# Adaptive FFN with experts: the low parts of h ahead of the turns of its rows

## The chip, the cores and the metric

The kernel runs on one core of one Trainium2 chip. The metric is the device time of one execution in microseconds. Five engines work side by side and meet at semaphores: TensorE (PE in the rows) multiplies 128x128 weights by up to 512 columns, VectorE (DVE) and ScalarE (ACT) work on tiles, GpSimd (POOL) does a little arithmetic and the indirect transfers, and SyncE (SP) issues the other DMAs in the order in which they are written.

## The reference

The input x has 8192 tokens of 512 numbers (128 batches of 64 tokens). Cut to what is computed:

```python
q_emb = relu(q @ W3 + b3)                                  # one row per batch
v_sum = sum(v, axis=1)
h = relu(((n * v + v_sum) * q_emb) @ W2 + b2)              # conditioned tokens
scores = softmax(h @ gate_w.T); topk_w, topk_i = top_k(scores, 6)      # 64 experts
buf = each expert's first 64 tokens (capacity 64), rows of h
y = (silu(buf @ w_gate) * (buf @ w_up)) @ w_down           # per expert, width 352
shared = (silu(h @ sw_gate) * (h @ sw_up)) @ sw_down       # all tokens, width 704
out = x + sum of y * weight over a token's experts + shared
```

## The kernel before, in words

**Precision.** A float32 product is made of three products in a shorter format: a value v is split into a high part (ScalarE's rounding copy) and a low part (VectorE's subtraction, `lower`, L743), and `three` (L1102 to L1104) adds high x high, high x low and low x high. For h these parts are `hh` and `hl`, each of four quarters `oc` of 128 features by the 512 tokens of a chunk.

**Stages.** The tokens are 16 chunks of 512. The first stage has a prologue (chunk 0, and the splitting of the shared weights, with GpSimd's part at L531) and eight bodies. A body `i` treats chunks b = 2i + 1, c = 2i + 2 and prepares d = 2i + 3; only the odd chunks' shared expert is done here, the even ones' follow in the second stage, beside the 32 pairs of experts. For each chunk:

- TensorE turns x (`transpose_x`, L1112); VectorE makes the conditioned input (`take_xt`, L764 to L783) and `xml` (`split_xm`), ScalarE `xmh`.
- TensorE multiplies by W2, one quarter of the features at a time (`cond_tile`, 48 matmuls a chunk in four tiles of 12). ScalarE takes each tile as h, relu and bias (`take_cond`, L597), and copies it to `hh`.
- VectorE turns each quarter of h into rows (`take_rows`, L796) for the table in DRAM from which the experts gather, and makes `hl` (`split_h`).
- TensorE multiplies h by the gate weights (`logits_raw`, L1136 and L1137, 8 matmuls of 512 columns), ScalarE copies the result to `lsb` (`take_lraw`), TensorE turns it (`logits`, L1147), and VectorE's `route` (L847 to L864) finds the six experts. `score` (L870 to L873) makes their weights from ScalarE's exp.
- For odd chunks, eleven gate and up tiles (`gu_tile`), with silu on ScalarE and `product` (L810) and `split_a` on VectorE between them, then four down tiles (`down_tile`, 17 matmuls each), which VectorE adds to x (`take_down`, L827 in this stage), and SP stores.
- The candidates of a body's two chunks are merged into each expert's first 64 in eight rounds (`merge`, L885 and L888, the last with L890).

**Order.** Everything is written out by hand: each engine's `body(i)` lists its steps, and its queue runs them strictly in that order. A step waits on semaphores for the others; a tile of PSUM is used again when its reader has signalled. SP's queue is in order too: a DMA that waits holds up all behind it. A TensorE unit at the high clock takes about 12 x 0.23 us for a `cond_tile` or `gu_tile`.

**What the prediction's steps touch.** VectorE's `split_h` and `body`; the opening lines of VectorE's queue; TensorE's `logits_raw`, called in the prologue for chunk 0 and in a body for b and for c; SP's `body`. ScalarE's `take_cond(n, oc)` waits for the turn and the low part of the same quarter of the chunk before, since h, `hh` and `hl` have one buffer each. The turned rows have one buffer as well (`hrow`): the first turn of a chunk waits until SP's stores of the last rows have landed, and `store_rows` waits for all four turns. `load_xr(v, j)` brings x for the sum of `take_down`, and has to wait until the buffer's last output is stored.

Of the kernel before, what the change touches and what calls it, by code (L numbers as in the profile page):

```python
# [21 lines left out]
def adaln_moe_ffn_kernel(nc, x, cond, W3, b3, W2, b2, gate_w, w_gate, w_up, w_down,  # L22
# [12 lines left out]
    NCH = T // CH  # L35
    J = CH // P
    KC = D // P
# [27 lines left out]
    with ctx:  # L65
# [26 lines left out]
        hh = keep("hh", [P, KC, CH], F32R)  # L92
        hl = keep("hl", [P, KC, CH], F32R)
# [253 lines left out]
        def _(sp):  # L347
# [95 lines left out]
            def body(i):  # L443
# [17 lines left out]
                if c < NCH:  # L461
                    store_hT(c // 2)
                    store_rows(c)
                    store_out(i, 0)
                    load_xr(i, 2)
                    store_out(i, 1)
                    keep_x(c)
# [273 lines left out]
        def _(dve):  # L741
# [57 lines left out]
            def split_h(n, oc):  # L799
                if n < NCH:  # L800
                    take_rows(n, oc)
                dve.wait_ge(s.hh_ready, KC * n + oc + 1)
                lower(hl[:, oc, :], h32[:, oc, :], hh[:, oc, :]).then_inc(s.hl_ready, 1)
# [92 lines left out]
            def body(i):  # L896
# [5 lines left out]
                score(a)  # L902
                split_h(b, 2)
                if i > 0:
                    merge(i - 1, 5)
                split_h(b, 3)
                if i > 0:
                    merge(i - 1, 6)
                    take_down(v - 1, 3)
                    merge(i - 1, 7)  # L910
                if not more:
# [37 lines left out]
                split_xm(d, 3)  # L949
                take_down(v, 0)  # L950
                take_down(v, 1)
                take_down(v, 2)

            def last_half(i):
# [90 lines left out]
            dve.wait_ge(s.pads_stored, 32)  # L1045
            split_h(0, 0)
            split_h(0, 1)
            take_xt(1, 2)
            split_h(0, 2)
            split_h(0, 3)  # L1050
            for j in range(J):
# [48 lines left out]
        def _(pe):  # L1100
# [29 lines left out]
            def logits_raw(n):  # L1130
                pe.wait_ge(s.hh_ready, KC * (n + 1))
                pe.wait_ge(s.hl_ready, KC * (n + 1))
                pe.wait_ge(s.cond_taken, KC * n + 3)
                o = bank[5]
                for k in range(KC):
                    nc.tensor.matmul(o[:, :], gw2[:, k, :], hl[:, k, :], start=(k == 0), stop=False)  # L1136
                    op = nc.tensor.matmul(o[:, :], gw2[:, k, :], hh[:, k, :], start=False, stop=(k == KC - 1))  # L1137
                op.then_inc(s.lraw_filled, 1)
# [242 lines left out]
```

## Time and profile before

| | us |
|---|---|
| median of 3 runs (range) | 1303.83 (1303.19 to 1304.71) |
| profiled execution | 1304.96 |
| its span | 1303.2 |
| TensorE busy in the span | 1262.3 (97%) |
| VectorE busy | 729.9 (56%) |
| ScalarE busy | 336.9 (26%) |
| TensorE idle before `logits_raw` | 18.4 |
| mean granted clock of TensorE, share of full | 0.986 |

The span is the time between the first and the last instruction; the rest of the profiled execution lies around it. Busy time of matmuls overlaps, so 97% is not the peak; what can be read from it is where TensorE is not busy. The first stage ends near 663 us, the second takes the rest.

### The profile page before, as it was taken

The page shows a single profiled execution, that of the slowest core. Times are in us where ns is not written, and L with a number is a line of the kernel's source. Part 1 is how long each engine was busy: PE and PEld are TensorE (multiplying, and loading weights), DVE is VectorE, ACT ScalarE, POOL GpSimd, SP SyncE. Part 2 cuts the span into 40 slices and gives each one's busy share as a digit, 9 for nine tenths or more (in the row PEclk, how much of TensorE's full clock was granted, in tenths as well). Part 3 has the DMA queues.
Part 4 walks back from the last instruction along what each step waited for, and adds up shares of the span by engine and source line. Part 5 has one row for each costly group of instructions (what it writes and reads, how often), then busy time and mean ns, then how long its engine had stood idle before and what let it go on. Part 6 is the DMA issues. An engine that isn't in the chain of part 4 may idle for free.

```text
span 1303.2 us, 15965 instructions
## 1 busy us (share of the span) xinstructions
PE 1262.3 (97%) x6104; PEld 935.7 (72%) x6104; DVE 729.9 (56%) x1524; ACT 336.9 (26%) x547; POOL 171.1 (13%) x129
## 2 busy tenths in 40 slices
PE   4879999999999999999999999999999999999999
PEld 3668888888888888887876666676666667666666
DVE  6789797979978797896743223232232232323322
ACT  3534233233424333342312011121121111211111
POOL 3320000000000000000001222222222222222221
PEclk7889999999999999999999999999999999999999
DMA  5531605344161532605755997987979889898852
GB/s 196 168 117 51 195 23 178 90 125 142 37 183 48 174 93 81 187 9 164 284 202 194 287 316 217 323 295 241 312 263 315 287 260 314 243 305 286 288 134 77
DMA packets 121453, 250.91 MB, mean 193 GB/s; under 512 B 18016, under 2 KB 50912, under 8 KB 119200
## 3 DMA queue, kind: packets, MB, share of 16 engines
q1 hardware_dynamic: 109888, 224.71, 51.0%
q0 software_dynamic: 11488, 25.17, 9.6%
q8 instruction: 49, 0.80, 0.2%
q14 instruction: 28, 0.23, 0.1%
HBM read 197.14 MB, written 61.10 MB: 198 GB/s over the span
## 4 chain that ended last, share of the span: by engine, by line
PE 96%; issue 2%; ACT 1%; DMA 1%; DVE 0%; SPq 0%
PE bank L1102 23%; PE bank L1104 22%; PE bank L1103 22%; PE bank L1300 12%; PE bank L1323 7%; PE bank L1112 2%; PE bank L1136 2%; PE bank L1137 1%; PE bank L1282 1%; PE bank L1197 1%; PE bank L1196 1%; PE bank L1309 1%; DMA stage<-in_L_cond_W_dram 1%; PE bank L1147 1%; ACT w2h L581 0%
## 5 line engine op out<-in xcount | busy, mean ns | idle before, releaser
L1102 PE MATMUL bank<-hh,gu 128*128 128x512 f32 x704 | 281.8, 400 | 0.0
L1104 PE MATMUL bank<-hh,gu 128*128 128x512 f32 x704 | 275.0, 391 | 0.0
L1103 PE MATMUL bank<-hl,gu 128*128 128x512 f32 x704 | 274.7, 390 | 0.0
L1102 PEld LDWEIGHTS bank<-hh,gu 128*128 128x128 f32 x704 | 132.8, 189 | 38.2 <-issue 12.8
L810 DVE TENSOR_TENSOR prod<-bank,prod 128x512 f32<-128x512 f32 x96 | 66.3, 690 | 165.7 <-PE bank L1104 139.6
L1104 PEld LDWEIGHTS bank<-hh,gu 128*128 128x128 f32 x704 | 132.3, 188 | 28.6
L1103 PEld LDWEIGHTS bank<-hl,gu 128*128 128x128 f32 x704 | 132.6, 188 | 25.4
L1102 PE MATMUL bank<-sdh,ah 128*128 128x512 f32 x320 | 126.8, 396 | 0.0
L581 ACT ACTIVATE ah<-prod 128x512 fp32r<-128x512 f32 x96 | 60.6, 632 | 251.3 <-DVE prod L810 251.3
L1103 PE MATMUL bank<-sdl,ah 128*128 128x512 f32 x320 | 124.7, 390 | 0.0
L1104 PE MATMUL bank<-sdh,al 128*128 128x512 f32 x320 | 124.7, 390 | 0.0
L536 POOL DMA_INDIRECT hg<-table,idx_pair x32 | 33.0, 1032 | 684.1 <-DVE idx_hi L1025 588.8
L1102 PE MATMUL bank<-xmh,w2h 128*128 128x512 f32 x256 | 103.7, 405 | 2.2 <-DVE xml L743 1.3
L617 ACT ACTIVATE prod<-bank 128x512 f32<-128x512 f32 x96 | 57.0, 594 | 172.4 <-PE bank L1104 172.2
L1104 PE MATMUL bank<-xmh,w2l 128*128 128x512 f32 x256 | 101.0, 395 | 0.0
L1103 PE MATMUL bank<-xml,w2h 128*128 128x512 f32 x256 | 100.9, 394 | 0.0
L1323 PE MATMUL bank<-wd,eactT 128*64 128x512 f32 (+1 forms) x384 | 89.6, 601 | 0.0
L1079 DVE TENSOR_SCALAR ysc<-bank,hg 64x512 f32<-64x512 f32 x64 | 48.0, 750 | 61.2 <-PE bank L1323 53.9
L1300 PE MATMUL bank<-wg,hgt 128*64 128x352 f32 x512 | 81.3, 459 | 0.0
L1300 PE MATMUL bank<-wu,hgt 128*64 128x352 f32 x512 | 81.2, 459 | 0.0
L597 ACT ACTIVATE h<-bank,b2c 128x512 f32<-128x512 f32 x64 | 44.0, 687 | 133.0 <-PE bank L1104 133.0
L1060 DVE TENSOR_TENSOR eact<-bank,esilu 128x352 f32<-128x352 f32 x32 | 16.8, 525 | 102.4 <-issue 96.4
(117 smaller groups left out, 1726.5 us busy)
## 6 DMA issues: line engine op xcount, KB each, us to landing
wg<-in_L_ffn_w_gate_dram SPq DMA_DIRECT2D x64, 704.0 KB, 8.0
wu<-in_L_ffn_w_up_dram SPq DMA_DIRECT2D x64, 704.0 KB, 10.3
wd<-in_L_ffn_w_down_dram SPq DMA_DIRECT2D x64, 512.0 KB
x<-in_x_dram SPq DMA_DIRECT2D x16, 1024.0 KB, 8.3
table<-hrow SPq DMA_DIRECT2D x64, 256.0 KB, 4.3
wd<-in_L_ffn_w_down_dram SPq DMA_DIRECT2D x64, 192.0 KB
out_dram<-outst SPq DMA_DIRECT2D x36, 256.0 KB, 4.5
hT<-h SPq DMA_DIRECT2D x8, 1024.0 KB, 3.9
```

What stands on the lines that cost most here:

```text
L536: nc.gpsimd.indirect_dma_start(out=hg[p % 3][:, :], out_offset=None, in_=table, in_offset=bass.IndirectOffsetOnAxis(ap=idx_pair[:, p:p + 1 ...
L581: return nc.scalar.activation(o, i, ACT.Copy)
L597: nc.scalar.activation(h32[:, oc, :], bank[5 + oc % 2][:, :], ACT.Relu, bias=b2c[:, oc:oc + 1]).then_inc(s.cond_taken, 1)
L617: nc.scalar.activation(prod[0:m, i % 2, :], bank[t % 3][0:m, :], ACT.Silu).then_inc(s.silu_ready, 1)
L810: nc.vector.tensor_tensor(prod[0:m, i % 2, :], bank[t % 3][up0:up0 + m, :], prod[0:m, i % 2, :], ALU.mult).then_inc(s.prod_ready, 1)
L1079: op = nc.vector.tensor_scalar(ysc[p % 3][rows, :], bank[6][rows, :], hg[p % 3][rows, at:at + 1], None, ALU.mult)
L1102: nc.tensor.matmul(o, st_h, mv_h, start=first_mm, stop=False)
L1103: nc.tensor.matmul(o, st_h, mv_l, start=False, stop=False)
L1104: return nc.tensor.matmul(o, st_l, mv_h, start=False, stop=last_mm)
L1112: op = nc.tensor.transpose(bank[3 + j % 2][:, k * P:(k + 1) * P], x32[:, n % 2, j, k * P:(k + 1) * P], ident[:, :])
L1300: op = nc.tensor.matmul(o[half, 0:I], hgt[:, k, half], w[p % 2][e][:, k * I:(k + 1) * I], start=(k == 0), stop=(k == KC - 1))
L1323: op = nc.tensor.matmul(bank[6][half, :], eactT[0:m, it, half], wd[e][0:m, it, :], start=(it == 0), stop=(it == IT - 1))
```

## The change

It has three parts. In `logits_raw` TensorE's four matmuls with `hh` come first, and each of the four with `hl` has a wait of its own. On VectorE `take_rows` is no longer part of `split_h`: in both halves of a body the four turns follow the four low parts, in the first half directly, in the second half after `take_down(v, 0)`; in the prologue the order stays as it was. Rounds 5, 6 and 7 of merging move from the first half of the next body to the end of the body, between and behind the down tiles. On SP `store_rows(c)` goes behind `load_xr(i, 2)`.

```diff
@@ SP, body
                 if c < NCH:
                     store_hT(c // 2)
-                    store_rows(c)
                     store_out(i, 0)
                     load_xr(i, 2)
+                    store_rows(c)
                     store_out(i, 1)
@@ VectorE, split_h
             def split_h(n, oc):
-                if n < NCH:
-                    take_rows(n, oc)
                 dve.wait_ge(s.hh_ready, KC * n + oc + 1)
@@ VectorE, body, first half
                 split_h(b, 2)
+                split_h(b, 3)
+                for oc in range(KC):
+                    take_rows(b, oc)
                 if i > 0:
-                    merge(i - 1, 5)
-                split_h(b, 3)
-                if i > 0:
-                    merge(i - 1, 6)
                     take_down(v - 1, 3)
-                    merge(i - 1, 7)
@@ VectorE, body, second half
                 take_down(v, 0)
+                for oc in range(KC):
+                    take_rows(c, oc)
                 take_down(v, 1)
+                merge(i, 5)
+                merge(i, 6)
                 take_down(v, 2)
+                merge(i, 7)
@@ TensorE, logits_raw
                 pe.wait_ge(s.hh_ready, KC * (n + 1))
-                pe.wait_ge(s.hl_ready, KC * (n + 1))
                 pe.wait_ge(s.cond_taken, KC * n + 3)
                 o = bank[5]
                 for k in range(KC):
-                    nc.tensor.matmul(o[:, :], gw2[:, k, :], hl[:, k, :], start=(k == 0), stop=False)
-                    op = nc.tensor.matmul(o[:, :], gw2[:, k, :], hh[:, k, :], start=False, stop=(k == KC - 1))
+                    nc.tensor.matmul(o[:, :], gw2[:, k, :], hh[:, k, :], start=(k == 0), stop=False)
+                for k in range(KC):
+                    pe.wait_ge(s.hl_ready, KC * n + k + 1)
+                    op = nc.tensor.matmul(o[:, :], gw2[:, k, :], hl[:, k, :], start=False, stop=(k == KC - 1))
```

TensorE, the product for chunk 0 with the instructions beside it, before (gw_67 is the gate weights, xmh and w2h are operands of `cond_tile`):

```order
L1104 MATMUL bank<-xmh,w2l 128x512
L1136 MATMUL bank<-hl,gw_67 128x512 [waits cond_taken,hl_ready,hh_ready]
L1137 MATMUL bank<-hh,gw_67 128x512
L1136 MATMUL bank<-hl,gw_67 128x512
L1137 MATMUL bank<-hh,gw_67 128x512
L1136 MATMUL bank<-hl,gw_67 128x512
L1137 MATMUL bank<-hh,gw_67 128x512
L1136 MATMUL bank<-hl,gw_67 128x512
L1137 MATMUL bank<-hh,gw_67 128x512
L1102 MATMUL bank<-xmh,w2h 128x512 [waits lraw_taken,cond_taken,xml_ready,xmh_ready]
```

and now:

```order
L1105 MATMUL bank<-xmh,w2l 128x512
L1136 MATMUL bank<-hh,gw_67 128x512 [waits cond_taken,hh_ready]
L1136 MATMUL bank<-hh,gw_67 128x512 x3
L1139 MATMUL bank<-hl,gw_67 128x512 [waits hl_ready] x4
L1103 MATMUL bank<-xmh,w2h 128x512 [waits lraw_taken,cond_taken,xml_ready,xmh_ready]
L1104 MATMUL bank<-xml,w2h 128x512
```

The wait for hl stood ahead of all eight; it now stands ahead of each of the last four.

VectorE, first half of body 0, chunk 1, from the end of its `route` to `take_xt` of chunk 2, before (hrow is the buffer of turned rows, h_54 is h, ez the exp):

```order
L796 STREAM_TRANSPOSE hrow<-h_54 128x512
L743 TENSOR_TENSOR hl<-h_54,hh 128x512
L796 STREAM_TRANSPOSE hrow<-h_54 128x512
L743 TENSOR_TENSOR hl<-h_54,hh 128x512
L870 TENSOR_REDUCE ssum<-ez 128x4
L871 RECIPROCAL rsum<-ssum 128x4
L873 TENSOR_TENSOR sc<-ez,rsum 128x256
L796 STREAM_TRANSPOSE hrow<-h_54 128x512
L743 TENSOR_TENSOR hl<-h_54,hh 128x512
L796 STREAM_TRANSPOSE hrow<-h_54 128x512
L743 TENSOR_TENSOR hl<-h_54,hh 128x512
L764 TENSOR_REDUCE vsum<-bank 128x8 x2
```

and now:

```order
L743 TENSOR_TENSOR hl<-h_54,hh 128x512 x2
L868 TENSOR_REDUCE ssum<-ez 128x4
L869 RECIPROCAL rsum<-ssum 128x4
L871 TENSOR_TENSOR sc<-ez,rsum 128x256
L743 TENSOR_TENSOR hl<-h_54,hh 128x512 x2
L796 STREAM_TRANSPOSE hrow<-h_54 128x512 x4
L764 TENSOR_REDUCE vsum<-bank 128x8 x2
```

The four turns have left the places ahead of the low parts and stand together behind the last of them.

VectorE, second half of body 0, chunk 2, from the last two quarters to the down tiles and the next `route`, before (outst is the output buffer of `take_down`):

```order
L796 STREAM_TRANSPOSE hrow<-h_54 128x512
L743 TENSOR_TENSOR hl<-h_54,hh 128x512
L796 STREAM_TRANSPOSE hrow<-h_54 128x512
L743 TENSOR_TENSOR hl<-h_54,hh 128x512
L743 TENSOR_TENSOR xml<-xm,xmh 128x4x128 x2
L743 TENSOR_TENSOR xml<-prod,xmh 128x4x128 x2
L827 TENSOR_TENSOR outst<-bank,outst 128x512 x3
L847 COPY lg<-bank 128x256
```

and now (first and cand are the merge's buffers):

```order
L743 TENSOR_TENSOR hl<-h_54,hh 128x512 x2
L743 TENSOR_TENSOR xml<-xm,xmh 128x4x128 x2
L743 TENSOR_TENSOR xml<-prod,xmh 128x4x128 x2
L825 TENSOR_TENSOR outst<-bank,outst 128x512
L796 STREAM_TRANSPOSE hrow<-h_54 128x512 x4
L825 TENSOR_TENSOR outst<-bank,outst 128x512
L883 MAX first<-cand 128x8
L886 MATCH_REPLACE cand<-first,cand 128x576
L883 MAX first<-cand 128x8
L886 MATCH_REPLACE cand<-first,cand 128x576
L825 TENSOR_TENSOR outst<-bank,outst 128x512
L883 MAX first<-cand 128x8
```

The turns of chunk c stand between the first two down tiles, two merge rounds between the next two, and the last round behind the third.

## Rows read from the trace of the kernel before

**Rows 1.** The page: shares of the span along the chain that ended last, by engine.

```profile
PE 96%; issue 2%; ACT 1%; DMA 1%; DVE 0%; SPq 0%
```

**Rows 2.** TensorE's waits: line, releaser, total us, times, longest us.

```profile
PE bank L1136 <- issue: 18.4, 10, 8.4
```

**Rows 3.** TensorE in time order: start us, duration us, instruction, [idle before, releaser]; the opening.

```profile
47.43 0.76 PE L1136 MATMUL bank<-hl,gw 128*128 128x512 f32 x1 [5.45 <-issue]
...
52.07 0.76 PE L1102 MATMUL bank<-xmh,w2h 128*128 128x512 f32 x1 [0.89 <-ACT lsb L581]
...
74.64 0.77 PE L1136 MATMUL bank<-hl,gw 128*128 128x512 f32 x1 [8.42 <-issue]
...
78.19 0.63 PE L1102 MATMUL bank<-hh,gu 128*128 128x512 f32 x1
...
81.56 0.60 PE L1147 MATMUL bank<-ident,lsb 128*128 128x128 f32 x4
...
87.49 1.03 PE L1112 MATMUL bank<-ident,x 128*128 128x128 f32 x8
```

**Rows 4.** TensorE in time order, around the product for chunk 4, body 1.

```profile
203.53 0.39 PE L1196 MATMUL bank<-sdh,ah 128*128 128x512 f32 x1
203.76 0.39 PE L1197 MATMUL bank<-sdl,ah 128*128 128x512 f32 x1
204.68 0.47 PE L1136 MATMUL bank<-hl,gw 128*128 128x512 f32 x1 [0.53 <-issue]
...
206.60 0.40 PE L1102 MATMUL bank<-sdh,ah 128*128 128x512 f32 x1
```

**Rows 5.** ScalarE and VectorE in time order, second half of body 1 and after.

```profile
201.06 0.63 ACT L581 ACTIVATE hh<-h 128x512 fp32r<-128x512 f32 x1
...
203.91 0.67 DVE L743 TENSOR_TENSOR hl<-h,hh 128x512 fp32r<-128x512 f32 x1
...
214.71 0.69 DVE L827 TENSOR_TENSOR outst<-bank,outst 128x512 f32<-128x512 f32 x1 [3.35 <-DMA outst<-in_x_dram]
...
217.68 0.42 DVE L847 COPY lg<-bank 128x256 f32<-128x256 f32 x1 [2.29 <-PE bank L1147]
...
220.46 0.69 ACT L597 ACTIVATE h<-bank,b2c 128x512 f32<-128x512 f32 x1
...
227.37 0.73 DVE L885 MAX8 first<-cand 128x8 f32<-128x576 f32 x1
```

**Rows 6.** Stretches: us, TensorE busy (matmuls), granted clock, DMA share, GB/s.

```profile
52.00:56.00 4.00, 3.93 (x10) 0.55 0.14 31
...
72.00:76.00 4.00, 1.36 (x3) 0.50 0.25 56
...
79.00:80.00 1.00, 1.00 (x5) 0.77 1.09 189
```

**Rows 7.** VectorE and ScalarE in the opening; last, GpSimd's L531: count, min/median/max ns, starts.

```profile
48.44 1.28 DVE L743 TENSOR_TENSOR xml<-prod,xmh 128x512 fp32r<-128x512 f32 x2
...
65.72 3.47 DVE L873 TENSOR_TENSOR sc<-ez,rsum 128x256 f32<-128x256 f32 x1
66.10 0.63 ACT L581 ACTIVATE hh<-h 128x512 fp32r<-128x512 f32 x1
...
69.11 1.08 DVE L796 STREAM_TRANSPOSE hrow<-h 128x512 f32<-128x512 f32 x1
70.04 2.98 DVE L743 TENSOR_TENSOR hl<-h,hh 128x512 fp32r<-128x512 f32 x1
...
L531 POOL TENSOR_TENSOR sdl<-stage,sdh x2: 3430/3521/3612, 65.5 to 68.9; 128x1536 fp32r<-128x1536 f32 x2
```

**Rows 8.** VectorE in body 0: `take_xt` of chunk 2, `route` of chunk 1, first product.

```profile
74.46 0.67 DVE L764 TENSOR_REDUCE vsum<-bank 128x8 f32<-128x512 f32 x1
...
82.20 0.42 DVE L847 COPY lg<-bank 128x256 f32<-128x256 f32 x1 [3.93 <-PE bank L1147]
...
86.90 0.69 DVE L810 TENSOR_TENSOR prod<-bank,prod 128x512 f32<-128x512 f32 x1
```

More of the change, by code:

```diff
@@ L1045, in _ @@
             dve.wait_ge(s.pads_stored, 32)
[L1046 to L1050, printed above, removed]
+            for oc in range(KC):
+                take_rows(0, oc)
+                split_h(0, oc)
+                if oc == 1:
+                    take_xt(1, 2)
             for j in range(J):
```

## The prediction, made before the changed kernel ran

> **What bounds the kernel now.** I read the page first. The chain that ended last is 96% TensorE [rows 1], so time is won only where TensorE waits or runs at its lower clock, and lost only where it starts to wait. The table of what TensorE waited for comes next: of its 1303.2 us it sat idle before the product of h with the gate weights (`logits_raw`, L1136) for 18.4 us in 10 cases [rows 2], and it lists no other wait after the one of 0.89 us ahead of 52.07 [rows 3], so none at all in the second stage. TensorE's timeline gives the cases: 5.45 us ahead of 47.43 (chunk 0), 8.42 us ahead of 74.64 (chunk 1) [rows 3], and eight short ones that make up the rest, 18.4 - 5.45 - 8.42 = 4.5 us: one in each of the seven bodies for chunk c, like the 0.53 ahead of 204.68 [rows 4], which make 3.7, and one for chunk 15, 0.8. The releaser is called "issue", but the matmul waits for the last piece of hl: VectorE's subtraction (L743) of 203.91 is the last before 204.68 [rows 5]. Last I asked for the granted clock by stretch: it is 0.50, which is 1.2 GHz, in the stretch from 72 to 76, and the mixed values 0.55 and 0.77 say that it came back to 2.4 GHz near 55.5 and near 79.5 [rows 6]. After each long wait TensorE worked for a while at the lower of its two clocks.
>
> **The change, part by part.**
>
> *TensorE's order in `logits_raw`.* The same eight matmuls; the four with hh go first and want only hh, then each hl matmul waits for its own quarter. No work added. Four waits are added where one stood; behind each stands all of TensorE's queue.
>
> *First product, chunk 0.* VectorE's order stays (turn, then low part, per quarter), so hl is complete when it was, just before 47.43. TensorE is free at 47.43 - 5.45 = 41.98 [rows 3], does the hh and two hl matmuls during the old wait, and the last two by about 47.8. Before, the product ended near 51, and `cond_tile(1, 0)` began at 52.07, when ScalarE had copied the logits. Now that copy is done near 48.6 and the next wait is what decides: xml of chunk 1, done at 48.44 + 1.28 = 49.7 [rows 7]. So that tile starts 2.3 us earlier, not 3.3. What those 2.3 us are worth hangs on the clock. At the low clock one 128x512 matmul takes 0.43 us of the queue (74.64 to 78.19 for eight, the first a little longer), at the high one 0.23 (203.53 to 203.76) [rows 3, 4]. The clock came back here at about 55.5 [rows 6]. If it comes back at the same moment, 2.3 us at the low clock are 5.4 matmuls, worth 5.4 x 0.23 = 1.2 us. If it never falls, TensorE does (55.5 - 49.8) / 0.23 = 25 matmuls by 55.5 instead of 8, worth 3.9. If the return comes later than it did, as little as 0.3. TensorE still stands idle for most of the time from 42 to 49.8, as it did before the clock was found low, so I take **1.2**.
>
> *Second product, chunk 1.* Here the order on VectorE changes. Before: a turn of 1.08 (0.93 from start to start, 69.11 to 70.04) stands ahead of each low part, and score (`sc`, L873) came at 65.72, just after GpSimd had begun its two subtractions of 3.43 and 3.61 us at 65.5 and 68.9; it took 3.47 instead of 0.42. The low part at 70.04 took 2.98 instead of 0.67, while the turn at 69.11, amid the second one, kept its 1.08 [rows 7]. Now, in the old time scale: route ends at 62.0 (65.72 less two turns, two low parts and two small instructions, 0.93, 0.6 and 0.3 apart), hl 0 and 1 run at 62.0 to 63.3, score ends by 64.3 and hl 2 by 65.0, all before GpSimd starts. hl 3 needs hh, at 66.10 + 0.63 = 66.7 [rows 7]; it meets the first subtraction, which ends at 68.9, and by the case of `sc` (in at 68.9, done at 69.19) it gets in between the two and is done by 69.4. TensorE, free at 74.64 - 8.42 = 66.2 [rows 3], does hh and hl 0 to 2 meanwhile and hl 3 until 69.7. The gate and up tile after it began at 78.19. With the 1.2 from above the new start is 68.5. The tile's 12 matmuls take 2.7 at the high clock, where before (78.19 to 81.56) they took 3.4: at the logits' transposes of 81.56 [rows 3] we stand at 71.2, **10.3 us earlier**, 1.2 of them the first product's. If the clock is lost at this wait too, and for as long as it was low for the work from 74.64 on (4.9 us, to 79.5), 11 matmuls at 0.43 cost 2.3 back: 8.0.
>
> The SBUF page of the Trainium skill (SBUF — State Buffer, section "Who interferes with whom") says that a VectorE instruction with two SBUF inputs contends with a GpSimd instruction that reads SBUF, and that the second to issue blocks until the first finishes. The rows of 65.72 and 70.04 agree, and so does the turn with its one input. The page does not say who comes next when both engines want the port at 68.9.
>
> *What is late next: VectorE in body 0.* The four turns now stand together between hl 3 and `take_xt(c, 0)`. hl 3 done at 68.2, turns 4 x 0.93 = 3.7, so 71.9; `take_xt` takes 3.8 (74.46 to 82.20 less 3.93 idle), so 75.7; route and one xml take 82.20 to 86.90 = 4.7, and the product of 0.69 is done at 81.1 [rows 8]. Tile 4 needs it (its bank is freed by it). TensorE gets there at 68.5 + 4 x 2.7 + 0.4 + 0.8 for the two groups of transposes = 80.6. So it waits 0.5; before, the same tile started at 87.49 + 0.8 + 2.7 = 91.0. Gain up to there 91.0 - 81.1 = 9.8. With the clock lost TensorE would come at 82.9 and not wait: 8.1. I take **9.3** for the opening, nearer to the first, since TensorE's pauses there are now under 2 us each. From the third product on VectorE waits for TensorE in this body, so nothing more is lost.
>
> *The seven short waits.* In the second half VectorE lacks two turns ahead of hl 2 and 3 and two ahead of 0 and 1. hh 3 is there at 201.06 + 0.63 = 201.7 [rows 5], so hl 3 is done at 202.4 instead of 204.6, and TensorE wants it only after down tile 0 (204.0) and four hh matmuls. From the start of the last down matmul, 203.76, to the next unit, 206.60, are 2.84 us for nine matmuls that take 9 x 0.23 = 2.05 [rows 4]: **0.8 each, 5.5 in all**. The last case: 0.8 and the same slow start, **1.1**; hh of chunk 15 has a whole down tile of cover, and no turn or merge stands in front any more.
>
> *Turns late in the second half.* hl 3 done at 202.4, four xml of 0.6 and `take_down(v, 0)` of 0.7 put them at 205.5 to 209.2; down tile 1 is full only at 205.8 + 17 x 0.23 = 209.7. That wait of VectorE for the down tile covers them. Who waits for them: ScalarE's next write of h, not before the next body's first tile is full, and SP, which stores the rows in four issues of 3.1 us together. These now follow `load_xr(i, 2)`, so they no longer delay the store and load of the residual, for which VectorE waited 3.35 us ahead of 214.71 [rows 5]. The load of x for the next body goes out some 1.2 us later; it has over 14 us to its transposes.
>
> *Merges 5, 6, 7.* The first two are 1.6 each (0.74 + 0.09 + 0.74 and the gaps, 227.37 on), the last 0.95 [rows 5]. 5 and 6 fit between down tiles 1 and 2 (3.9 us apart, less 0.7 for `take_down`), 7 ends near 215.4; the route of chunk c begins when its logits are there, now 216.8 (217.68 less 0.8). VectorE sat 2.29 idle ahead of it [rows 5]. So they cost nothing there and free 4.2 us in the first half, which carried no TensorE wait. Without that cover, each us beyond 1.3 would push the route, exp on ScalarE, the take of tile 1 behind it, and `cond_tile(b, 3)` after some 1.7 us more of slack (that take ended at 220.46 + 0.69 = 221.15 [rows 5], the tile began near 222.9, three units after down tile 2: 206.60 + 2 x 3.9 + 3 x 2.75 + 0.35).
>
> *First half of a body.* Turns of b move behind hl 3 and ahead of `take_down(v - 1, 3)`: same sum, nothing on TensorE's path. **0**, bounds 0 and 0.1 per body.
>
> **Sum.** 9.3 + 5.5 + 1.1 = 15.9; the profiled execution was 1304.96 us, so 1289.1. The median of the runs shown is 1.1 below that execution; the same step from it gives 1287.9. I take 1288.5.
>
> **Rivals.**
> 1. *hl 3 of chunk 1 falls behind GpSimd's second subtraction.* It is done near 71.8 instead of 68.2, and the turns, `take_xt` and route shift with it: tile 4 at 84.7, gain 6.3, in all 12.9: **1291.5**. For: the low part of 70.04 waited the whole second subtraction out [rows 7]. Against: `sc` at 65.72 stood where hl 3 will stand, and got in between.
> 2. *The clock stays up through the first wait.* 1.7 to 2.7 more from the opening: **1286**. For: TensorE has six matmuls to do in what was one wait. Against: the low clock after both waits.
> 3. *The short waits stay.* Something other than hl 3 holds TensorE after the down tile (a restart after the change of bank, say). Then 5.5 + 1.1 shrink to 1 or so: **1294**. For: the profile calls the releaser "issue". Against: hl's ends at 203.91 + 0.67 and at 204.68 match to 0.1.
> 4. *Slower: turns and merges bunched before the route.* One mechanism: VectorE reaches the route of chunk c late, each of seven bodies. It has 1.3 us of slack and the chain behind 1.7; the loss begins at 3.0 us late, and outweighs the 15.9 at 3.0 + 15.9 / 7 = 5.3 us late. With 7 us late it is 7 x 4.0 = 28 - 16: **1316**. For: 3.7 of turns and 4.2 of merges now stand in a stretch that had none. Against: the stretch had 3.35 and 2.29 us of idle time behind the last two down tiles alone [rows 5], and VectorE now enters it 2 us earlier.
>
> **How the numbers follow.** Chances: forecast 0.66, rival 1 0.12, rival 2 0.12, rival 3 0.07, rival 4 0.03. The likeliest case alone spans 1286 to 1291; rivals 1 to 3 and the unknown clock make it 1284 to 1294.5, which leaves out part of rival 3 and all of rival 4. No change can be told within 0.2%, 2.6 us, of 1303.8. Faster than that hold the first four cases, 0.95; a mixture of rival 3 and a lesser opening could end within it, 0.02; slower 0.03.
>
> **What would show it.** In the profile after: TensorE's waits at `logits_raw` fall from 18.4 us to under 3; none in the seven bodies; the logits of chunk 1 near 71; a short wait at gate and up tile 4 of body 0; `sc` at 0.42; the turns in a row of four with VectorE idle between them and down tile 1; the wait for the residual load gone or shorter. I am wrong if the clock spends over 10 us at 0.50 after 41 us, if hl 3 of chunk 1 ends after 71, or if waits appear at `cond_tile(b, 3)` or at gate and up tiles 4 and 6 of later bodies.

## The result

| | before | after |
|---|---|---|
| median (range) of 4 runs, us | 1304.27 (1303.19 to 1304.82) | 1284.78 (1284.01 to 1285.64) |
| profiled execution, us | 1304.96 | 1285.33 |
| its span, us | 1303.2 | 1283.5 |
| mean granted clock | 0.986 | 0.992 |

The ratio is 0.9852, with a 95% interval of 0.9835 to 0.9869: 19.5 us faster by the medians, 19.6 by the two profiled executions. The forecast was 1288.5, with 1284.0 to 1294.5 as its range, so the measured median lies 0.8 us inside the lower end.

**The profile after.** What TensorE waited for, in the same columns as [rows 2] (L1136 is now the matmul with hh, L1139 the one with hl, L1103 the first matmul of a `cond_tile`; the whole table):

```profile
PE bank L1113 <- DVE vsum L771: 10.4, 1, 10.4
PE bank L1205 <- DMA w3s<-in_L_cond_W_dram: 5.0, 1, 5.0
PE bank L1103 <- DVE xml L743: 3.3, 2, 1.9
PE bank L1136 <- ACT hh L581: 2.0, 2, 1.4
PE bank L1139 <- DVE hl L743: 1.9, 2, 1.0
PE bank L1113 <- DVE xm L779: 1.3, 1, 1.3
PE bank L1210 <- ACT condT L581: 0.5, 1, 0.5
```

The 18.4 us in 10 cases are 3.9 in four, two in each of the first two products. The eight short waits have gone. One wait has taken the place of another: the tile after the first product stood 0.89 us for the copied logits and now stands 1.93 for xml of chunk 1. TensorE's timeline in the opening answers to [rows 3]:

```profile
43.68 1.20 PE L1136 MATMUL bank<-hh,gw 128*128 128x512 f32 x4 [1.44 <-ACT hh L581]
44.71 1.01 PE L1139 MATMUL bank<-hl,gw 128*128 128x512 f32 x3
46.76 0.50 PE L1139 MATMUL bank<-hl,gw 128*128 128x512 f32 x1 [1.03 <-DVE hl L743]
49.19 0.77 PE L1103 MATMUL bank<-xmh,w2h 128*128 128x512 f32 x1 [1.93 <-DVE xml L743]
...
63.82 1.19 PE L1136 MATMUL bank<-hh,gw 128*128 128x512 f32 x4 [0.56 <-ACT hh L581]
64.85 0.84 PE L1139 MATMUL bank<-hl,gw 128*128 128x512 f32 x3
66.59 0.50 PE L1139 MATMUL bank<-hl,gw 128*128 128x512 f32 x1 [0.90 <-DVE hl L743]
69.69 0.60 PE L1149 MATMUL bank<-ident,lsb 128*128 128x128 f32 x4
...
79.31 0.50 PE L1103 MATMUL bank<-hh,gu 128*128 128x512 f32 x1
```

In both products seven matmuls run before hl 3 is there, and one is left over for it. The logits of chunk 1 are turned at 69.69 where it was 81.56 [rows 3]: 11.9 us. Gate and up tile 4 of body 0 (79.31) starts a little late: the last matmul ahead of it starts at 79.03 and the next could follow 0.23 later, but the product on VectorE ends at 78.57 + 0.68 = 79.25. The clock by stretch, columns as in [rows 6]:

```profile
42.00:49.00 7.00, 2.79 (x10) 1.00 0.86 302
49.00:53.00 4.00, 3.81 (x10) 0.57 0.72 163
60.00:68.00 8.00, 6.53 (x32) 1.00 0.07 16
```

There is one short stretch at the low clock, until about 52.5, where the kernel before had one until 55.5 and one until 79.5. The product for chunk 4, in body 1, answers to [rows 4]:

```profile
191.12 0.39 PE L1199 MATMUL bank<-sdl,ah 128*128 128x512 f32 x1
191.35 1.07 PE L1136 MATMUL bank<-hh,gw 128*128 128x512 f32 x4
192.25 1.07 PE L1139 MATMUL bank<-hl,gw 128*128 128x512 f32 x4
193.16 0.39 PE L1103 MATMUL bank<-sdh,ah 128*128 128x512 f32 x1
```

From the last down matmul to the next unit it is 193.16 - 191.12 = 2.04 us, against 206.60 - 203.76 = 2.84 [rows 4]. VectorE and SP in the same second half, which answer to [rows 5]:

```profile
189.08 0.69 DVE L743 TENSOR_TENSOR hl<-h,hh 128x512 fp32r<-128x512 f32 x1 [1.31 <-ACT hh L581]
...
192.70 3.80 DVE L796 STREAM_TRANSPOSE hrow<-h 128x512 f32<-128x512 f32 x4
192.81 0.34 SPq L391 DMA_DIRECT2D out_dram<-outst  x1
...
194.83 0.33 SPq L386 DMA_DIRECT2D outst<-in_x_dram  x1
196.53 3.10 SPq L373 DMA_DIRECT2D table<-hrow  x4
197.22 0.69 DVE L825 TENSOR_TENSOR outst<-bank,outst 128x512 f32<-128x512 f32 x1 [0.71 <-PE bank L1199]
...
204.23 0.42 DVE L845 COPY lg<-bank 128x256 f32<-128x256 f32 x1 [1.57 <-PE bank L1149]
```

The turns fill what was a wait for down tile 1, the merges what was a wait for the residual and for down tile 2; 1.57 us of idle time are left ahead of the route. The residual load goes out 2.0 us after the store of the output (194.83 after 192.81). In the opening, [rows 7] is answered by these (the last gives GpSimd's two subtractions):

```profile
60.18 0.42 DVE L871 TENSOR_TENSOR sc<-ez,rsum 128x256 f32<-128x256 f32 x1
...
63.14 0.63 ACT L581 ACTIVATE hh<-h 128x512 fp32r<-128x512 f32 x1
...
63.80 2.74 DVE L743 TENSOR_TENSOR hl<-h,hh 128x512 fp32r<-128x512 f32 x1 [2.03 <-ACT hh L581]
66.46 3.88 DVE L796 STREAM_TRANSPOSE hrow<-h 128x512 f32<-128x512 f32 x4
...
L531 POOL TENSOR_TENSOR sdl<-stage,sdh x2: 3490/3738/3985, 62.5 to 65.9; 128x1536 fp32r<-128x1536 f32 x2
```

Score is down from 3.47 to 0.42 us. hl 3 still stands beside GpSimd's first subtraction and takes 2.74 us, but it ends at 66.5, just behind that subtraction; GpSimd's second one is the longer for it, 3.99 us against 3.61 before.

**Where the 19.6 us came from.** The starts of the same TensorE instructions, before less after:

| place | before, us | gained by then |
|---|---|---|
| logits of chunk 0 turned | 56.53 | 2.95 |
| logits of chunk 1 turned | 81.56 | 11.87 |
| ranks of body 0 turned | 96.57 | 11.67 |
| last matmul of down tile 0, then of down tile 1, body 0 | 127.0, 133.4 | 11.67, 12.44 |
| ranks turned, bodies 1, 2, 3 | | 12.64, 13.70, 14.70 |
| bodies 4, 5, 6 | | 15.70, 16.71, 17.71 |
| body 7 | 625.34 | 19.63 |
| last down tile | 1299.34 | 19.63 |

So 11.7 us in the opening, 1.0 in each of six steps from body to body (0.8 at the product of chunk c, 0.2 at the next of chunk b), 1.9 in the last step (0.8, and 1.1 at chunk 15), and nothing lost or gained in the second stage.

### The profile page after: what moved, and what is told of

It is laid out like the page before. It is cut to its first block, busy times and chain, and to the rows that moved or that the text cites. A ratio compares the mean times of both kernels' runs of the same rounds, so it can differ in the third digit from the quotient of the medians.

```text
span 1283.5 us, 15965 instructions
## 1 busy us (share of the span) xinstructions
PE 1255.9 (98%) x6104; PEld 932.9 (73%) x6104; DVE 728.4 (57%) x1524; ACT 337.2 (26%) x547; POOL 171.7 (13%) x129
## 4 chain that ended last, share of the span: by engine, by line
PE 96%; DVE 2%; ACT 1%; DMA 1%; issue 1%; SPq 0%
PE bank L1103 23%; PE bank L1105 23%; PE bank L1104 22%; PE bank L1302 12%; PE bank L1325 7%; PE bank L1113 2%; PE bank L1284 1%; PE bank L1199 1%; PE bank L1198 1%; PE bank L1139 1%; PE bank L1136 1%; PE bank L1311 1%; DMA stage<-in_L_cond_W_dram 1%; PE bank L1149 1%; DVE hl L743 0%
## 5 line engine op out<-in xcount | busy, mean ns | idle before, releaser
L1103 PE MATMUL bank<-hh,gu 128*128 128x512 f32 x704 | 281.5, 400 | 0.0
L1103 PEld LDWEIGHTS bank<-hh,gu 128*128 128x128 f32 x704 | 132.5, 188 | 38.4 <-issue 12.8
L1103 PE MATMUL bank<-sdh,ah 128*128 128x512 f32 x320 | 126.7, 396 | 0.0
L1103 PE MATMUL bank<-xmh,w2h 128*128 128x512 f32 x256 | 103.6, 405 | 3.3 <-DVE xml L743 3.3
L743 DVE TENSOR_TENSOR hl<-h,hh 128x512 fp32r<-128x512 f32 x96 | 66.9, 724 | 29.8 <-ACT hh L581 29.4
```

Of the source, the lines that this page charges most:

```text
L743: return nc.vector.tensor_tensor(o, full, high.bitcast(F32), ALU.subtract)
L1103: nc.tensor.matmul(o, st_h, mv_h, start=first_mm, stop=False)
```

## The experiments

All are compared with the kernel before on the same chip; "gained by" numbers are the starts of TensorE's instructions as in the table above, from one profiled execution each, always against the profiled execution before (1304.96 us, which is 0.7 above the median of its four runs and 1.7 above the 1303.29 of 15 later runs of the same kernel). The code shown is cut to what changed, with its array views shortened.

**Which half of the change works, and where.** e1 takes TensorE's order alone:

```diff
--- the kernel before
-                pe.wait_ge(s.hl_ready, KC * (n + 1))
...
-                    nc.tensor.matmul(o, gw2[:, k, :], hl[:, k, :], start=(k == 0), stop=False)
-                    op = nc.tensor.matmul(o, gw2[:, k, :], hh[:, k, :], start=False, stop=(k == KC - 1))
+                for k in range(KC):
+                    nc.tensor.matmul(o, gw2[:, k, :], hh[:, k, :], start=(k == 0), stop=False)
+                for k in range(KC):
+                    pe.wait_ge(s.hl_ready, KC * n + k + 1)
+                    op = nc.tensor.matmul(o, gw2[:, k, :], hl[:, k, :], start=False, stop=(k == KC - 1))
```

> The kernel before with the new matmul order in logits_raw alone; VectorE and SP as before. Theory: every short wait was for the last quarter of hl, and the four hh matmuls (0.9 us) cover a lateness of 0.5 to 0.8 us, so the products of chunk c, of chunk b and of chunk 15 gain as in the changed kernel: 8 us after the opening. In the opening the first product gains 3 us, the second still waits for hl 3 behind the turns and GpSimd: its logits come near 75 instead of 69.7, 6.5 us before those of the kernel before. In all 14 to 15 us faster, about 1290. Rival A (the change of VectorE's order is what cures the short waits): they stay, and the gain is 6 to 7 us. Rival B (the matmuls gain from standing in groups with one operand): the gain per body would stand without any wait going.

Measured: 1291.36 us, ratio 0.9906 (0.9889 to 0.9922). Gained 3.96 us at the logits of chunk 0, 5.51 at those of chunk 1, and from there 1.0 per body like the changed kernel, 13.5 in all. No short wait is left. The theory holds for the bodies and rival A falls. In the opening the two gains were 1 us off in opposite directions: at the first product the granted clock stayed at 1.00 (from 42 to 67), while behind the second wait it was low (0.62 from 67 to 76). The second product waits for the low parts between the turns:

```profile
62.82 1.19 PE L1135 MATMUL bank<-hh,gw 128*128 128x512 f32 x4 [0.56 <-ACT hh L581]
...
69.37 0.80 PE L1138 MATMUL bank<-hl,gw 128*128 128x512 f32 x1 [4.89 <-DVE hl L743]
```

e2 takes the rest without it:

```diff
--- the changed kernel
-                for k in range(KC):
-                    nc.tensor.matmul(o, gw2[:, k, :], hh[:, k, :], start=(k == 0), stop=False)
-                for k in range(KC):
-                    pe.wait_ge(s.hl_ready, KC * n + k + 1)
-                    op = nc.tensor.matmul(o, gw2[:, k, :], hl[:, k, :], start=False, stop=(k == KC - 1))
+                pe.wait_ge(s.hl_ready, KC * (n + 1))
+                for k in range(KC):
+                    nc.tensor.matmul(o, gw2[:, k, :], hl[:, k, :], start=(k == 0), stop=False)
+                    op = nc.tensor.matmul(o, gw2[:, k, :], hh[:, k, :], start=False, stop=(k == KC - 1))
```

> The changed kernel with the old logits_raw (hl and hh in turns behind one wait for all); VectorE and SP as changed. Theory: hl is ready before TensorE comes in every body, so the short waits go as well and the 8 us after the opening are gained here too. Opening: nothing at the first product (it waits 5.4 us for hl as before), at the second hl is ready near 69.4, its logits near 74: 7.5 us. In all 15 to 16 us faster, about 1289; together with e1 it says that the two halves overlap after the opening and add only in it. Rival B (grouping of operands): no gain per body, 7 to 8 us in all.

Measured: 1290.90 us, ratio 0.9903 (0.9887 to 0.992). Nothing gained at chunk 0, 5.8 at chunk 1, again 1.0 per body, 13.8 in all. TensorE's waits for hl:

```profile
PE bank L1137 <- issue: 8.8, 2, 5.4
```

Rival B falls: the matmuls gain the same per body in either order. Either half alone cures every product after the opening; only in the opening do both count: 5.5 and 5.8 alone, 11.7 together. The expected 7.5 us at chunk 1 were 1.7 too many, since the clock was low again for the start of the second product's work (0.57 from 69 to 73).

**Four waits or one.**

```diff
--- the changed kernel
-                for k in range(KC):
-                    pe.wait_ge(s.hl_ready, KC * n + k + 1)
+                pe.wait_ge(s.hl_ready, KC * (n + 1))
+                for k in range(KC):
                     op = nc.tensor.matmul(... hl[:, k, :] ...)
```

> The changed kernel with one wait for all of hl between the four hh and the four hl matmuls, in place of four. Theory: the separate waits matter in the opening alone, where three hl matmuls run while hl 3 is late: three of them fall behind it in both products, 3 x 0.23 each at full clock, 1.0 to 1.5 us slower than the changed kernel in all, and nothing per body. Rival: the four waits cost TensorE something in each product; then the bodies are faster than now.

Measured: 1287.75 us (1285.09 to 1288.38), ratio 0.9877 (0.9862 to 0.9892), 3 us more than the changed kernel's median. Per body it is the same (1.0), so the separate waits cost nothing there. At the logits of chunk 0 it had gained 1.58 instead of 2.95, at those of chunk 1 9.39 instead of 11.87. The three matmuls behind hl 3 explain 0.7 each as expected. The rest is the clock, which was low there for longer:

```profile
44.00:56.00 12.00, 9.21 (x25) 6.59 (x24) 5.06 (x8) 5.75 (x11) 5.33 (x3) 0.57 0.66 178
```

(The columns between the busy time of matmuls and the clock are those of the other engines.) 0.57 over 12 us is 10 us at the low clock, where the changed kernel had 3.4. One of the four runs took 1285.09 us at a mean clock of 0.992, that of the changed kernel, where the other three had 0.989; so the clock's share of the 3 us may be larger than the profiled execution (1287.61) shows; the short run was not profiled.

**The moves that the forecast had priced at nothing: merges and SP's order.**

```diff
--- the changed kernel, VectorE
                 split_h(b, 2)
+                if i > 0: merge(i - 1, 5)
                 split_h(b, 3)
+                if i > 0: merge(i - 1, 6)
                 (turns) ... take_down(v - 1, 3)
+                if i > 0: merge(i - 1, 7)
...
                 take_down(v, 1)
-                merge(i, 5)
-                merge(i, 6)
                 take_down(v, 2)
-                merge(i, 7)
```

> The changed kernel with merge rounds 5, 6 and 7 back in the first half of the next body (5 between low parts 2 and 3, 6 behind 3, 7 behind take_down). Theory: they lie beside TensorE's work in either place, 1284.8 within 0.5 us, and no wait of TensorE beside those of the opening. Rival: 4.2 us of merges before take_xt and the route delay the first product of a body, TensorE waits at gate and up tile 4 in seven bodies; at 0.3 us each 2 us slower.

Measured: 1285.19 us (1284.61 to 1286.89), ratio 0.9864 (0.9847 to 0.988); gained 11.61 at body 0 and 19.56 at body 7, against 11.67 and 19.63. No further wait of TensorE. The theory holds: the merges' place is worth nothing that can be told.

```diff
--- the changed kernel, SP
                     store_hT(c // 2)
+                    store_rows(c)
                     store_out(i, 0)
                     load_xr(i, 2)
-                    store_rows(c)
```

> The changed kernel with SP's store_rows(c) back ahead of store_out(i, 0). Theory: SP now waits there for the four turns (about 3.8 us later than the sum of down tile 0), so the residual load comes 5 us or more later, VectorE waits for it before down tile 2 and merge 7 and the route start about 2 us late; the chain to cond_tile(b, 3) has about 1.7 us of slack behind VectorE's 1.6, so TensorE loses 0 to 0.5 us per body: 1284.8 to 1288. Rival: nothing at all, since the store of the output was never what limited the load.

Measured: **1314.95 us** (1311.89 to 1318.14), ratio 1.0098 (1.0074 to 1.0121), slower than the kernel before. I had expected at most 3 us of loss, and the rival none; it is 30. TensorE's table has one new row, the largest:

```profile
PE bank L1103 <- ACT h L597: 20.8, 7, 4.0
```

The chain in body 0, in time order on SP, VectorE, ScalarE and TensorE:

```profile
115.73 3.80 DVE L796 STREAM_TRANSPOSE hrow<-h 128x512 f32<-128x512 f32 x4
...
119.56 3.11 SPq L373 DMA_DIRECT2D table<-hrow  x4
...
122.71 1.29 SPq L391 DMA_DIRECT2D out_dram<-outst  x1
...
128.71 0.35 SPq L386 DMA_DIRECT2D outst<-in_x_dram  x1
...
131.68 0.69 DVE L825 TENSOR_TENSOR outst<-bank,outst 128x512 f32<-128x512 f32 x1 [7.57 <-DMA outst<-in_x_dram]
...
135.94 0.67 ACT L597 ACTIVATE h<-bank,b2c 128x512 f32<-128x512 f32 x1
```

and at its end:

```profile
136.66 0.79 PE L1103 MATMUL bank<-xmh,w2h 128*128 128x512 f32 x1 [3.95 <-ACT h L597]
```

SP stands for the four turns until 119.5, needs 3.1 us to issue the rows, and the output's store, now behind a megabyte of rows, takes 6.0 us from issue until the load that waits for it goes (128.71 after 122.71; 4.5 to 5.5 in the next six bodies, and 2.0 to 2.1 in those of the changed kernel). The store behind the rows was slow in the kernel before too, 4.1 to 4.8 us; what e4 adds to it is that SP first stands for the turns. VectorE waits 7.57 us for the residual, so merge 7 and the route (133.19) are 6 us late, exp and `take_cond` with them, and the fourth `cond_tile` waits. Seven such waits are 20.8 us. Behind three of them, in bodies 0, 1 and 6, the granted clock was low (0.64 from 137 to 141, 0.57 from 218 to 222 and from 614 to 618), which is 3.4 us at 0.50 each time; by the price that e6 finds below, that is some 5 us. The two profiled executions are 26.6 us apart, and 27.7 counted from body 0 on, since e4's opening was 1.1 us the faster; about 2 us of them are left that I did not take apart. This is the chain of rival 4 of the forecast, at its place; what set it off is the order on SP, not the sum of VectorE's work.

The converse, SP's order alone in the kernel before (the same three lines moved the other way):

```diff
--- the kernel before, SP
                     store_hT(c // 2)
-                    store_rows(c)
                     store_out(i, 0)
                     load_xr(i, 2)
+                    store_rows(c)
```

> The kernel before with SP's store_rows(c) behind load_xr(i, 2), and nothing else changed. Theory: in the kernel before the turns are done before down tile 0, so the order costs nothing that TensorE sees: 1303.5 within 0.5 us; only VectorE's wait for the residual ahead of take_down(v, 2) (3.4 us) goes or shrinks. That would say that the move on SP is worth nothing by itself and 27 to 30 us once the turns stand behind take_down(v, 0). Rival: the residual's earlier arrival is worth something alone, 1 us or more.

Measured: 1303.16 us (1301.43 to 1304.93, 10 runs), ratio 1.0002 (0.9992 to 1.0011): nothing. VectorE's waits for the residual fall, in the column of totals from 29.0 us in 9 cases to

```profile
DVE outst L827 <- DMA outst<-in_x_dram: 4.6, 2, 3.6
```

so the move does what it says and pays only where the turns are late (e4 against the changed kernel).

**The opening.** The three waits around the first product, filled with matmuls of no use:

```diff
--- the changed kernel, TensorE, prologue
             cond_tile(0, 3)
+            fill(6)                       # matmul(bank[7], w2h[:, 0, 0:P], w2l[:, 0, :])
             logits_raw(0)                 # with fill(4) ahead of its last matmul
+            fill(8)
```

> The changed kernel with 18 matmuls of 512 columns on constant operands into a PSUM bank that nobody reads, in TensorE's three waits around the product of chunk 0 (6, 4 and 8); their results are not used. Theory: the 3.4 us at 0.50 after 49.1 come from the idle stretches ahead; kept busy, TensorE stays at full clock and the eight matmuls done there take 0.23 instead of 0.43 us: 1.6 us faster than the changed kernel, 1283.2, with clock 1.00 from 43 on. Rival: the clock falls anyway or the filling lengthens the waits: 1285 to 1286.

Measured: 1284.36 us, ratio 0.9854 (0.9838 to 0.9869), not to be told from the changed kernel. By the profile the clock did what the theory says:

```profile
42.00:50.00 8.00, 7.03 (x28) 4.61 (x26) 8.00 (x15) 5.09 (x9) 0.00 (x0) 1.00 0.74 257
50.00:53.00 3.00, 2.91 (x13) 2.31 (x13) 0.09 (x1) 1.63 (x4) 2.85 (x1) 1.00 0.93 215
```

The clock stays at 1.00, and the `cond_tile` takes 2.81 us from its start to the logits' transposes (50.20 to 53.01) where the changed kernel takes 4.39 (49.19 to 53.58): 1.6 us, the expected size. But the tile started 1.0 us later, which leaves 0.6 (gained by body 0: 12.25 against 11.67). That is not the filling: the eight end at 50.11, and xml of chunk 1, for which the tile waits, ends at 50.10, where it ended at 49.08 in the changed kernel. VectorE was late there because one low part of chunk 0 stood beside GpSimd's subtraction, 36.18 + 3.21 here and 35.84 + 0.68 in the changed kernel, in an order of instructions that is the same in both.

Two other runs show the price without any filling. In the profiled executions of e1 and e4, whose opening is that of the changed kernel up to this tile, the clock stayed at 1.00 too. The tile and the logits behind it in e4:

```profile
49.59 0.47 PE L1103 MATMUL bank<-xmh,w2h 128*128 128x512 f32 x1 [1.94 <-DVE xml L743]
...
52.43 0.60 PE L1149 MATMUL bank<-ident,lsb 128*128 128x128 f32 x4
```

These are 2.84 us again (e1: 49.73 to 52.57), against 4.39 in the changed kernel and 4.40 in e3 (49.25 to 53.65). So the fall at this tile came in two of four profiled executions with one and the same opening; it is worth 1.6 us, and which of the two comes is luck as far as these runs tell.

The turns of chunk 0 behind its low parts and the xml of chunk 1:

```diff
--- the changed kernel, VectorE, prologue
             for oc in range(KC):
-                take_rows(0, oc)
                 split_h(0, oc)
                 if oc == 1:
                     take_xt(1, 2)
             for j in range(J):
                 split_xm(1, j)
+            for oc in range(KC):
+                take_rows(0, oc)
```

> The changed kernel with the turns of chunk 0 moved behind its four low parts and the xml of chunk 1, in the prologue. Theory: hl 3 of chunk 0 and xml of chunk 1, which TensorE waits for at 46.8 and 49.2, come earlier by at least the four turns (3.7 us), until ScalarE's xmh copies (done at 45.7) set the limit; cond_tile(1, 0) starts near 46.4, 2.8 us earlier, and the low clock of 49.1 to 52.5 may go as well (1.7 us). 1280.3 to 1282. Rival: the turns come in the way of what follows (route of chunk 0, take_cond of chunk 1 that waits for them), and the gain is under 1 us.

Measured: 1282.82 us (1282.65 to 1283.33), ratio 0.9844 (0.9831 to 0.9858). The ratios' intervals overlap; the medians are 2.0 us apart, and by the profile the gain is 2.4 us (14.03 at body 0 against 11.67). The tile after the first product starts behind a wait of 1.07 instead of 1.93, hl 3 of chunk 0 is no longer waited for, and there is no low clock after 43. The gain is of the expected kind but smaller than the 2.8 to 4.5 us asked for: the tile starts 1.6 us earlier (47.58 against 49.19) and not 2.8, since VectorE now stands 1.99 us for hh ahead of 38.03, where a turn was. The clock adds 1.5 us at the logits of chunk 0; the move need not be its cause, as e1 and e4 show.

From there, W2 split in four pieces on ScalarE and GpSimd:

```diff
--- the kernel of e5
-        pieces = [([(w2v, stage)], [(w2h, w2l, stage)])]                       # one copy, one subtraction
+        pieces = [([(w2v, stage)], [(w2h[:, k], w2l[:, k], stage[:, k]) for k in range(KC)])]
...
-            pe.wait_ge(s.stage_split_l, 1)
+            pe.wait_ge(s.stage_split_l, splits_before[1])
```

> The kernel of e5 with the splitting of W2 cut into four copies on ScalarE and four subtractions on GpSimd. VectorE's first xml subtractions stood 6.2 us at 17 to 23 us because GpSimd's one subtraction of 5.5 us reads SBUF at the same time, and TensorE waited 10.8 us for what follows. Theory (the one who comes second waits for the end of the instruction that runs, and gets in before the next): VectorE loses at most one quarter, about 1.4 us, per instruction; cond_tile(0, 0) starts near 25.2 instead of 28.9, and the kernel takes about 1279.5, 3.5 us less than e5. Rival (GpSimd's next instruction goes first when both wait): VectorE still waits for all four, no gain over e5, 1282.8.

Measured: 1281.45 us, ratio 0.9829 (0.9815 to 0.9842). The gain over e5 is 1.4 us by the medians and 0.9 by the profiles, not 3.5; `cond_tile(0, 0)` starts 1.5 us earlier (27.29 against 28.80). VectorE's stands were 6.2 us for two xml subtractions behind GpSimd's single one; now they are

```profile
14.29 1.25 DVE L773 TENSOR_TENSOR vsum<-vsum,qT 128x8 f32<-128x8 f32 x1
...
16.07 3.41 DVE L785 TENSOR_TENSOR xm<-xm,vsum 128x512 f32<-128x512 f32 x2
19.40 2.60 DVE L745 TENSOR_TENSOR xml<-xm,xmh 128x512 fp32r<-128x512 f32 x2
```

So VectorE does get in between two instructions of GpSimd, each time after one of them, and the rival falls. What I had not counted: GpSimd now begins at 14.0 instead of 16.4, when VectorE has three more such instructions to do, and each of them waits as well.

And the other shared weights by single rows of k, the same edit on the remaining pieces:

```diff
--- the kernel of e8
-                [(whole[0], whole[1], cols), (tail[0], tail[1], ...)]
+                [(whole[0][k], whole[1][k], cols[k]) for both k] + [(tail[0], tail[1], ...)]
...
-        [(sdh[:, 0:3], sdl[:, 0:3], v)]
+        [(sdh[:, k], sdl[:, k], v[:, k]) for k in range(3)]
```

> The kernel of e8 with the shared weights split in smaller pieces too: one of the k rows at a time in place of two or three. Theory: the waits of VectorE for a GpSimd subtraction (2.6 us at 29.8, 2.7 us at the hl 3 of chunk 1) shrink to at most 1.5 us each, TensorE gains 0.5 to 1.5 us in the opening over e8. Rival: more instructions on ScalarE and GpSimd, each with its own start, cost as much as the shorter waits give: the same as e8 within 0.5 us.

Measured: 1280.99 us (1280.06 to 1281.74), ratio 0.9828 (0.9815 to 0.9842): the same as e8 within what can be told, as its rival said. It is the fastest version that ran, 22.3 us below the kernel before in the same session by the medians; the changed kernel was 19.5 below in its own. The intervals of the two ratios still touch.

## Why the prediction was right, and which sizes were off

**The bound and the place of the waits.** Right: every wait at the product that was named has shrunk or gone, and the second stage moved as a whole. Of the signs, one missed: the waits at `logits_raw` are 3.9 us, not under 3. No sign of being wrong appeared (3.4 us at 0.50 after 41 us, hl 3 of chunk 1 done at 66.5, no wait at `cond_tile(b, 3)` nor at later gate and up tiles).

**First product, 1.2 us expected, 2.95 measured.** The bound is the one that was named, xml of chunk 1, and the tile's start is 2.9 us earlier than before, not 2.3 (49.19 where 49.8 was worked out). The 0.6 us are not the change's doing: they come from a low part of chunk 0 that met GpSimd's subtraction in the profile before and slipped in ahead of it in the profile after. Before:

```profile
35.65 3.38 DVE L743 TENSOR_TENSOR hl<-h,hh 128x512 fp32r<-128x512 f32 x1
```

and after:

```profile
35.84 0.68 DVE L743 TENSOR_TENSOR hl<-h,hh 128x512 fp32r<-128x512 f32 x1
```

At the low clock they are worth 0.6 x 0.23 / 0.43 = 0.3 us. The mis-sized factor was the clock: I let it come back when it had come back before, at 55.5, and it came back at 52.5, after a fall that came 3.8 us later. 3 us at the high clock in place of the low are 13 matmuls in place of 7, 1.4 us. 1.2 + 0.3 + 1.4 is the 2.9 measured. It was the case between the forecast and rival 2. A clock that never falls was put at 3.9 us, and in e1 and e4, where it did not fall here, the logits of chunk 0 gained 3.96 and 4.10. Which case an execution gets is luck as far as these runs tell: two of four had the fall.

**The profile before is a slow one.** In the profile of e10, where nothing in the opening had been changed, TensorE's first wait was 3.54 instead of 5.45 us, the mean clock from 42 to 80 was 0.82 instead of 0.73, and the ranks of body 0 were turned 3.5 us earlier. That execution took 1301.43 us, the shortest of its ten, and the one before 1304.96. So of the opening's 11.7 us a us or two belong to the pair of executions and not to the change; the medians, 19.5 us apart, are the safer measure of the whole.

**Second product.** 9.1 us expected between the two logits (10.3 less 1.2), 8.9 measured. hl 3 got in between GpSimd's two subtractions (63.80 + 2.74 = 66.5, second subtraction from 65.9), as `sc` had done at 65.72. What the Trainium skill leaves open (SBUF — State Buffer, section "Who interferes with whom"), who comes next when both want the port, was read from that row and came out so; rival 1 fell, and e8 shows the same with four pieces. The clock was not lost at this wait.

**VectorE late in body 0.** 0.5 us expected at gate and up tile 4, 0.2 measured (11.87 gained at the logits of chunk 1, 11.67 at the ranks of body 0).

**The product of chunk c.** 0.8 us each, measured 0.76 to 0.82. The reason given was right, but both halves of the change were counted on, and e1 and e2 show that one would do.

**The product of chunk b, 0 expected, 0.2 measured.** This step failed, by 1.3 us in six bodies. The product for chunk 5 did wait in the kernel before; I looked at matmuls alone, where no idle time is listed ahead of it, since the ends of the transposes, which the profile models, cover it. The weight loads show it. Of the kernel before, TensorE's loads and VectorE:

```profile
229.32 1.02 PEld L1112 LDWEIGHTS bank<-ident,x 128*128 128x128 f32 x8
230.56 0.19 PEld L1136 LDWEIGHTS bank<-hl,gw 128*128 128x128 f32 x1 [0.22 <-issue]
```

```profile
229.81 0.68 DVE L743 TENSOR_TENSOR hl<-h,hh 128x512 fp32r<-128x512 f32 x1
```

hl 3 ends at 230.49 and the load follows at 230.56. The same gain of 0.2 us stands in e1 and in e2 (at the logits of chunk 3, 6.52 against 6.33 and 6.79 against 6.60). In all the bodies gave 7.96 us where 6.6 were forecast.

**Merges.** Nothing, as forecast (e3).

**SP's order.** The forecast named it as a side effect and gave it no price. What it missed is that the turns' late place is safe only with that move: 30 us by e4, against 0 for the move alone by e10. The bounds for "turns late" should have held that case. Rival 4 had the right chain and asked for VectorE to be over 3 us late from its own work; in e4 a wait of 7.6 us for a load did it.

In sum: opening 9.3 expected, 11.7 measured; chunk c 5.5 and 5.6; chunk b 0 and 1.3; chunk 15 1.1 and 1.1. The sum fell 3.8 us short of the gain between the two profiled executions; that the forecast held is owed to the room below it that the unknown clock had been given.

## What to carry to other kernels

A wait on the last part of an operand is best split where the parts are used, and put behind the work that needs none of them; a second cure for the same wait adds nothing once the first has covered it, so price each alone and at each place. When work is moved later on one engine, follow what a DMA queue has behind its wait for that work: a store in order ahead of a store and load pair can turn free work into the longest wait of the kernel. Look at weight loads as well as at matmuls before a unit is called free of waits. And profile one kernel more than once before a few us in its opening are read as the work of a change.

## What the runs showed of the hardware that I had not expected

- Instructions of VectorE and GpSimd that both read two SBUF operands took turns in these traces: behind the GpSimd instruction that ran, VectorE's went ahead of the next one each time (65.72 in the kernel before, 63.80 in the changed one, and the three rows of e8), while STREAM_TRANSPOSE beside GpSimd kept its 0.93 to 0.97 us from start to start.
- A store of 256 KB took 2.0 to 2.1 us from its issue to the load that waits for it in seven bodies of the changed kernel, where no rows are ahead of it, and with four stores of rows issued just ahead of it 4.1 to 4.8 us in the kernel before and 4.5 to 6.0 in e4.
- Single executions differ in the opening, with the same order of instructions on every engine, in two ways: by where the clock falls and returns (at the tile behind the first product in the changed kernel and e3, not in e1 and e4), and by whether one low part of VectorE slips in ahead of a subtraction of GpSimd (0.68 us at 35.84 in the changed kernel, 3.21 at 36.18 in e6). e10's ten runs lie between 1301.43 and 1304.93 us.
